# A ternary feedforward stage: its first bias as a product of four rounded rows, row scales for four tiles at once, x kept in SBUF, and longer lags in each engine's order

## The reference, cut to what matters

```python
def rms_norm(x): return x * rsqrt(mean(x * x, -1) + EPS)
def act_quant(x):
    scale = 127.0 / clip(max(abs(x), -1), 1e-05)
    return clip(round(x * scale), -128.0, 127.0) / scale
def weight_quant(w):
    scale = 1.0 / clip(mean(abs(w)), 1e-05)
    return clip(round(w * scale), -1.0, 1.0) / scale
def bitlinear158(x, w, b):
    return act_quant(rms_norm(x)) @ weight_quant(w).T + b
h = silu(bitlinear158(x, w1, b1))      # 2048 x 2048
h = gelu(h)                            # the exact form
h = layer_norm(h, ln_g, ln_b)
x = layernorm(x + bitlinear158(h, w2, b2))
```

## Time and profile before

| | |
|---|---|
| Median of three runs | 2302.09 us (2299.7 to 2304.48) |
| Span of the profiled execution | 2297.3 us |
| Stage `ternary_feedforward` in it | from about 1976.6 us to the end |
| Busy over the whole span | PE 81%, DVE 65%, ACT 41%, POOL 23% |
| Mean granted TensorE clock | 0.902 of full |

### The profile page before, as it was taken

The page is one execution under the profiler, slowest core; times in us unless marked ns, Lnnn a source line. Parts: engine busy times, 40 slices in busy tenths (PEclk is TensorE's granted clock), DMA queues, the critical chain, the costliest instruction groups (busy, mean ns, idle before and its releaser), DMA issues. The chain is left out here.

```text
span 2297.3 us, 32982 instructions
## 1 busy us (share of the span) xinstructions
PE 1871.9 (81%) x12321; PEld 1405.0 (61%) x12321; DVE 1483.0 (65%) x2816; ACT 941.1 (41%) x1589; POOL 520.8 (23%) x515
## 2 busy tenths in 40 slices
PE   2337989874667999999999959999984998478886
PEld 2225555521446999999999948787763776234443
DVE  8846877577673665666566645657662776467775
ACT  1004555620322444444444433333434111477774
POOL 0032322045010001010000001100100887234442
PEclk9958999965888999999999979999987999789897
DMA  5089999323742222212222232322214113600100
GB/s 201 0 125 144 142 142 140 48 101 121 227 140 70 61 65 59 81 58 66 74 74 64 60 108 102 111 74 74 100 57 177 49 48 105 243 10 28 37 14 23
DMA packets 145837, 208.45 MB, mean 91 GB/s; under 512 B 13520, under 2 KB 84048, under 8 KB 143248
## 3 DMA queue, kind: packets, MB, share of 16 engines
q1 hardware_dynamic: 136720, 189.57, 31.8%
q10 hardware_dynamic: 8960, 16.78, 1.9%
HBM read 159.82 MB, written 46.22 MB: 90 GB/s over the span
## 5 line engine op out<-in xcount | busy, mean ns | idle before, releaser
L452 DVE TENSOR_REDUCE a_rowmax<-a_ring 128x2 f32<-128x512 f32 x256 | 164.9, 687 | 82.6 <-PE a_ring L534 80.6
L1594 DVE TENSOR_TENSOR f_hid<-f_gate,f_gu 128x256 f32<-128x256 f32 x264 | 108.3, 420 | 162.1 <-ACT f_gate L1466 159.4
L1466 ACT ACTIVATE f_gate<-f_gu 128x256 f32<-128x256 f32 x264 | 98.7, 382 | 274.5 <-PE f_gu L1332 187.2
L2431 PE MATMUL e_py<-e_kv,e_toep 128*128 128x320 f32 x640 | 174.9, 437 | 4.7 <-DVE e_kv L2455 4.7
L397 ACT ACTIVATE a_prob<-a_sT 128x1024 f32<-128x1024 f32 x128 | 130.6, 1026 | 74.1 <-PE a_sT L523 73.7
L2431 PEld LDWEIGHTS e_py<-e_kv,e_toep 128*128 128x128 f32 x640 | 122.9, 192 | 56.5 <-issue 6.5
L1345 PE MATMUL f_gu<-f_lowh,f_bg 128*128 128x256 f32 x704 | 141.3, 283 | 5.3 <-POOL f_lowl L1251 5.0
L1332 PE MATMUL f_gu<-f_xhi,f_wg 128*128 128x256 f32 x704 | 129.8, 282 | 0.0
L1332 PE MATMUL f_gu<-f_xhi,f_wu 128*128 128x256 f32 x704 | 129.1, 281 | 0.0
L1345 PEld LDWEIGHTS f_gu<-f_lowh,f_bg 128*128 128x128 f32 x704 | 115.8, 191 | 9.8 <-POOL f_lowl L1251 5.2
L1599 DVE TENSOR_TENSOR f_hl<-f_hid,f_hh 128x768 fp32r<-128x768 f32 (+2 forms) x90 | 84.7, 941 | 55.9 <-ACT f_hh L1512 54.8
(11 more groups left out here) (379 smaller groups left out, 4967.5 us busy)
## 6 DMA issues: line engine op xcount, KB each, us to landing
f_entry<-in_WdT SPq DMA_DIRECT2D x89, 256.0 KB, 2.8
d_staging<-in_w SPq DMA_DIRECT2D x16, 1024.0 KB, 5.5
a_qs<-parts SPq DMA_DIRECT2D x96, 128.0 KB, 6.3
a_ks<-parts SPq DMA_DIRECT2D x96, 128.0 KB, 6.9
parts<-a_hi SPq DMA_DIRECT2D x16, 512.0 KB, 8.7
parts<-a_lo SPq DMA_DIRECT2D x16, 512.0 KB, 8.9
e_toep<-lags SPq DMA_DIRECT2D x32, 256.0 KB
f_entry<-in_Bg SPq DMA_DIRECT2D x89, 64.0 KB, 1.8
```

The source lines that it names most:

```text
L452: dve.tensor_reduce(rowmax[:, s % 2, :, e * SLOTS + j], ring[n % RING][:, :].rearrange("p (q t) -> p q t", t=T), AX.X, ALU.max, negate=Tru ...
L1466: act.activation(gate[:, i % 2, :], gu[n % 3][:, 0, :], ACT.Silu).then_inc(s_["gate_ready"], 1)
L1594: dve.tensor_tensor(hid[:, j, :], gate[:, i % 2, :], gu[n % 3][:, 1, :], ALU.mult).then_inc(s_["hid_ready"], 1)
L2431: last = pe.matmul(py[n % RING][:, 0:DIAG * BS], toep[:, h % 3, (t - j) * P:(t - j + 1) * P], kv[:, h % 2, :, j, :], start=(j == 0), stop= ...
```

## The change: what it does, and the diff

- The bias of the first product: b1 is loaded on 4 partitions. ACT and DVE split it once into a rounded fp32r part and its remainder (`g_bhigh`, `g_bpart`). The number per row is split likewise into four columns (`g_lcols`), which PE transposes to four rows (`g_lrows`, through `g_pq1` and an ACT copy, once for four tiles). The bias is then a product of 4 rows by 512 columns in fp32r, four matmuls per tile, in place of the 128-row fp32 product. `g_diag` is gone.
- Row maxima, roots and scales of x are made for a group of four tiles at once: `group_peaks`, `group_scales`, four squares in a row on ACT, one root on POOL.
- x is loaded by SP in four transfers of four tiles and stays in SBUF. The ring and its refills are gone.
- `g_hc` has four buffers instead of two. Steps run from -3 to 23 instead of 0 to 22.
- The order of PE in a step: bias and matmuls of W(s-1); the transposed rows of a group (at s = -1, 3, 7, 11); q(s); the four transposed groups of tile s-5; O(s-6).
- The order of ACT in a step: squares of four tiles of x (at s = -3, 1, 5, 9); the copy of `g_lrows` (at s = -1, 3, 7, 11); on even s silu(s-1), `g_q1f`(s), gelu(s-2), on odd s gelu(s-2), `g_q1f`(s), silu(s-1); squares about the mean (s-3); four `g_q2f` copies (s-5); squares of `g_hc` (s-4).
- The order of DVE in a step: scales of a group; mean and gain product (s-3), no longer behind the squares about the mean; addition and statistics (s-7); scales and rounding of `g_hc` (s-5); `g_xq`(s); shift and maximum of `g_hc` (s-4); result (s-7); maxima of a group.
- The order of POOL in a step: root of a group of x; root of s-5; root of s-7; b2 added to x (s-1); root of s-3.

```diff
-    DEPTH = 6
+    GT = 4
+    NG = NT // GT
     QB = INNER // 512
-    XT = 8
+    LAST = 8
+    STEPS = range(-3, NT + LAST)
...
+    def group_at(s, lead):
+
+        t = s + lead
+        return t // GT if 0 <= t < NT and t % GT == 0 else None
...
+        lcols = mk.sb("g_lcols", [P, NT, 4])
+        lrows = mk.sb("g_lrows", [4, 2, GT * P], F32R)
...
-        hc = mk.sb("g_hc", [P, 2, INNER])
+        hc = mk.sb("g_hc", [P, 4, INNER])
...
+                def load_x(g):
+                    sp.dma_start(xt[:, tiles(g), :], io["x5"][g * GT * P:(g + 1) * GT * P, :].rearrange("(n p) f -> p n f", p=P)
+                                 ).then_inc(got_x[g], 16)
...
+                load_x(1)
...
+                        pool.wait_ge(s_["ssq2"], t + 1)
+                        root(row2[:, t, :], 0, INNER, s_["root2"])
+                    t = tile_at(s, 7)
+                    if t is not None:
+                        pool.wait_ge(s_["var_ready"], t + 1)
+                        root(stats[:, t, :], 7, 1.0, s_["root_ready"])
+                    t = tile_at(s, 1)
+                    if t is not None:
+                        pool.wait_ge(s_["q1_ready"], t + 1)
+                        if t == 0:
+                            pool.wait_ge(s_["b2_in"], 16)
+                        pool.tensor_tensor(xt[:, t, :], xt[:, t, :], b2[:, :], ALU.add).then_inc(s_["b2_added"], 1)
+                    t = tile_at(s, 3)
                     if t is not None:
...
                 for s in STEPS:
-                    t = tile_at(s, 4)
+                    g = group_at(s, 3)
+                    if g is not None:
...
+                        if g == 0:
+                            act.wait_ge(s_["b1_in"], 16)
+                            act.activation(bhigh[:, :], brow[:, :], ACT.Copy).then_inc(s_["bhigh_ready"], 1)
+                    g = group_at(s, 1)
+                    if g is not None:
+                        act.wait_ge(s_["turned"], turn_at["f", g] + 1)
+                        if g >= 2:
+                            act.wait_ge(s_["h_done"], (g - 1) * GT)
+                        act.activation(lrows[:, g % 2, :], pq1[0:4, :], ACT.Copy).then_inc(s_["turn_read"], 1)
+                    for first, lag in ((True, 1), (False, 2)) if s % 2 == 0 else ((True, 2), (False, 1)):
+                        t = tile_at(s, lag)
+                        if t is not None:
+                            silu(t) if lag == 1 else gelu(t)
+                        t = tile_at(s, 0) if first else None
+                        if t is not None:
+                            act.wait_ge(s_["turned"], turn_at["q", t] + 1)
+                            if t >= 2:
+                                act.wait_ge(s_["h_done"], t - 1)
+                            act.activation(q1f[:, t % 2, :, :], pq1[:, :].rearrange("p (k t) -> p k t", k=KT), ACT.Identity,
+                                           bias=minus[:, :]).then_inc(s_["turn_read"], 1)
+                    t = tile_at(s, 3)
...
                 for s in STEPS:
                     t = tile_at(s, 1)
                     if t is not None:
-                        pe.wait_ge(s_["q1_ready"], t + 1)
-                        if t >= 1:
-                            pe.wait_ge(s_["q1f_ready"], t)
...
                         if t >= 1:
                             pe.wait_ge(s_["silu_done"], t)
                         else:
                             pe.wait_ge(s_["got_w1"], 16 * KT)
+                            pe.wait_ge(s_["bpart_ready"], 1)
+                        pe.wait_ge(s_["turn_read"], turn_at["q", t] + 1)
                         for n in range(QB):
-                            pe.matmul(p1[:, n * 512:(n + 1) * 512], diag[:, t % 2, :], b1[:, n * 512:(n + 1) * 512],
-                                      start=True, stop=False)
+                            pe.matmul(p1[:, n * 512:(n + 1) * 512], lrows[:, t // GT % 2, t % GT * P:(t % GT + 1) * P],
+                                      bpart[:, n * 512:(n + 1) * 512], start=True, stop=False)
+                        for n in range(QB):
+                            for j in range(KT):
+                                last = pe.matmul(p1[:, n * 512:(n + 1) * 512], q1f[:, t % 2, j, :], w1[:, j, n * 512:(n + 1) * 512],
+                                                 start=False, stop=(j == KT - 1))
+                        last.then_inc(s_["h_done"], 1)
+                    g = group_at(s, 1)
+                    if g is not None:
+                        pe.wait_ge(s_["lift_ready"], g + 1)
+                        claim(("f", g))
+                        for i in range(GT):
+                            last = pe.transpose(pq1[0:4, i * P:(i + 1) * P], lcols[:, g * GT + i, :], keep["ident"][:, :])
+                        last.then_inc(s_["turned"], 1)
+                    t = tile_at(s, 0)
+                    if t is not None:
+                        pe.wait_ge(s_["q1_ready"], t + 1)
+                        claim(("q", t))
+                        for j in range(KT):
+                            last = pe.transpose(pq1[:, j * P:(j + 1) * P], xq[:, t % 2, j * P:(j + 1) * P], keep["ident"][:, :])
+                        last.then_inc(s_["turned"], 1)
                     t = tile_at(s, 5)
...
-                    t = tile_at(s, 5)
+                    t = tile_at(s, 6)
...
+                    of = tiles(g)
+                    dve.wait_ge(s_["root1"], g + 1)
+                    dve.wait_ge(s_["max1"], g + 1)
+                    xs.step(dve.tensor_tensor(top[:, of], peak[:, of], xroot[:, of], ALU.mult))
+                    xs.step(dve.tensor_scalar(top[:, of], top[:, of], 1e-5, None, ALU.max))
+                    dve.tensor_scalar(back1[:, of], top[:, of], 1 / 127.0, wmean[:, 0:1], ALU.mult, ALU.mult).then_inc(s_["x_steps"], 1)
+                    xs.n += 1
+                    xs.step(dve.reciprocal(inv1[:, of], top[:, of]))
+                    dve.scalar_tensor_tensor(fore1[:, of], inv1[:, of], 127.0, xroot[:, of], ALU.mult, ALU.mult
+                                             ).then_inc(s_["fore_ready"], 1)
+                    xs.step(dve.tensor_scalar(lift[:, of], inv1[:, of], wfac[:, :], None, ALU.mult))
+                    xs.step(dve.tensor_copy(lhigh[:, of], lift[:, of]))
+                    high = lhigh[:, of].bitcast(F32)
+                    dve.tensor_copy(lcols[:, of, 0:2], high.unsqueeze(2).broadcast_to([P, GT, 2])).then_inc(s_["x_steps"], 1)
+                    xs.n += 1
+                    xs.step(dve.tensor_tensor(lcols[:, of, 2:4], lift[:, of].unsqueeze(2).broadcast_to([P, GT, 2]),
+                                              high.unsqueeze(2).broadcast_to([P, GT, 2]), ALU.subtract))
+                    dve.sem_inc(s_["lift_ready"], 1)
...
                 for s in STEPS:
-                    t = tile_at(s, 1)
+                    g = group_at(s, 2)
+                    if g is not None:
+                        group_scales(g)
+                    t = tile_at(s, 3)
                     if t is not None:
+                        dve.wait_ge(s_["gelu_done"], t + 1)
+                        dve.tensor_scalar(hs[:, t, 1:2], hs[:, t, 0:1], -1.0 / INNER, None, ALU.mult).then_inc(s_["mean_ready"], 1)
...
+                        dve.scalar_tensor_tensor(hc[:, t % 4, :], ha[:, t % 3, :], hs[:, t, 1:2], gain[:, :], ALU.add, ALU.mult
+                                                 ).then_inc(s_["gained"], 1)
+                    t = tile_at(s, 7)
                     if t is not None:
...
+                    t = tile_at(s, 0)
+                    if t is not None:
+                        dve.wait_ge(s_["fore_ready"], t // GT + 1)
+                        if t >= 2:
+                            dve.wait_ge(s_["turned"], turn_at["q", t - 2] + 1)
+                        dve.tensor_scalar(xq[:, t % 2, :], xt[:, t, :], fore1[:, t:t + 1], ROUND, ALU.mult, ALU.add
+                                          ).then_inc(s_["q1_ready"], 1)
...
+                    g = group_at(s, 3)
+                    if g is not None:
+                        group_peaks(g)
+                        if g == 0:
+                            dve.wait_ge(s_["bhigh_ready"], 1)
+                            dve.scalar_tensor_tensor(bpart[:, :], bhigh[:, :].bitcast(F32), takes[:, 1:2], brow[:, :],
+                                                     ALU.mult, ALU.add).then_inc(s_["bpart_ready"], 1)
```

More of the change, by code:

```diff
@@ L2506, in ternary_feedforward, with tile_at @@
     NT = N // P
-    DEPTH = 6
+    GT = 4
+    NG = NT // GT
     QB = INNER // 512
-    XT = 8
+    LAST = 8
+    STEPS = range(-3, NT + LAST)
     own = keep["ternary"]
     wmean, winv = own["wmean"], own["winv"]
+    def tile_at(s, lag):
+        t = s - lag
+        return t if 0 <= t < NT else None
+    def group_at(s, lead):
+        t = s + lead
+        return t // GT if 0 <= t < NT and t % GT == 0 else None
+    turn_at = {}
+    for s in STEPS:
+        if group_at(s, 1) is not None:
```

(31 more changed lines are left out.)

176 lines of the change are left out of this document (75 added, 101 removed).

## The result

The changed kernel takes 2344.8 us (median of four runs, 2342.21 to 2345.81), the kernel before 2301.44 us beside it (four runs, 2299.7 to 2304.48): a ratio of 1.0176, 95% interval [1.0161, 1.0192]. It is 1.8% slower. The forecast was 2351. The profiled execution has a span of 2342.6 us against 2297.3, and a mean granted clock of 0.888 against 0.902.

A forecast was written before the change was run, and what follows sets the result against it. No engine was full; a chain of waits through PE and ACT bound the kernel. W(5) to W(15) +35, start +3 and end +11 made +49 on 2297.3: span 2346, median 4.8 higher, 2351 us; range 2332 to 2372.

The forecast's parts named there:

- The ring: W(5) to W(15): each step one closed loop of PE's and ACT's parts, 33.7 us per two tiles against 34 before.
- The clock: PE behind its idle stretch runs transposes and O at half clock, adding 2.7 us per step.
- The bias: On PE, four fp32r matmuls at 0.93 us per tile replace bias passes of 9.7 us per two tiles.
- The rival of a dear one: Four-row fp32r bias matmuls run as the old passes, 2.7 us more in ten steps: 2378 us, chance 0.05.
- The port: POOL's addition of b2 holds up DVE and makes `g_xq` late: 1.0 us per odd step, hidden in even ones.
- Four tiles at once: ACT's `g_lrows` copy costs 2 us each in steps 7 and 11, 4 in all; squares and group scales nothing.
- The start: Loads and first tiles up to the end of W(5): +3 us, from -4 to +10.
- The end: From W(15) to the end of the span: about 77 us instead of 66.2, +11, between 2 and 14.
- The rival "each engine at its own busy time": Transposes do not hold PE; each engine runs at its busy time, 12.9 us per tile: 2270 us, chance 0.07.

The follow-up runs named there:

- e3: The changed kernel with the four bias matmuls of each tile done four times; 2407.18 us, ratio 1.0444 to the kernel before.
- e1: The changed kernel with O(s-6) ahead of the transposed groups of tile s-5 in PE's order; 2306.7 us, ratio 1.0008 to the kernel before.
- e5: The changed kernel with PE making the second transposed group fourteen times for tiles 1 to 11; 2324.1 us, ratio 1.0102 to the kernel before.
- e7: e1 with DVE making `g_xq`(s) right behind the gain product and POOL's addition of b2 last; 2309.09 us, ratio 1.0032 to the kernel before.
- e2: The changed kernel with PE making the second transposed group ten times for tiles 1 to 11; 2336.31 us, ratio 1.0129 to the kernel before.
- e6: The changed kernel with POOL's addition of b2 last in a step, behind the root of s-3; 2345.52 us, ratio 1.0189 to the kernel before.
- e9: e8 with PE making the second transposed group six times for tiles 1 to 11; 2277.49 us, ratio 0.9881 to the kernel before.
- e8: e7 with ACT's `g_lrows` copy behind gelu and DVE's split of b1 behind the first group scales; 2300.21 us, ratio 0.9994.
- e4: The kernel before, its order kept, with b1 and `g_diag` rounded to fp32r and the low part left out; 2289.3 us, ratio 0.9928.

## Why the prediction was right, point by point

- **The ring** held. It was forecast that W(5) to W(15) becomes one closed loop of PE's and ACT's parts, 204.5 us; it took 200.2. e3 shows that PE's work lies in it undiminished, and e1 that O is what was put in series: 29.7 us of the ten tiles go with it, clock included. Each part fits too: from W's end to the third group the sum has 8.5 us for an even step (7.8 and the first copy), and all five take 8.5. PE's idle time ahead of the third group was to be 5.3 and 6.7 us and is 5.7 to 7.2; ACT's even chain was to be 7.8 and is 7.75 (2071.04 to 2078.79).
- **The clock** was right in kind and too large in size: 2.7 per step, measured 2.1 (after against e5, 1.3 to 2.8). The transposes lose 0.74, where 0.9 was forecast, and O the other 1.3, where 1.8 was; O was sized by the slow rows of the tail, mean 5.44, and took 3.8 to 5.3 in the loop (15 of its 16 matmuls), since PE regained full speed within it. The Trainium skill's rule on recurring idle stretches ("TensorE: Matmul & The Clock Gate", "HAM oscillation — how this bites in real kernels") agrees with after, where every round starts slow behind 5.7 to 7.2 us of idle. The shorter stretches do not fit so simply: in e7 and e2, behind 2.3 and 2.5 us, the transposes could still run at full speed (1.23) and the slow work came behind them, and behind 1.8 us in the next step of e2 none came.
- **The bias** starts the next block 1.13 us later, not 0.93: 4-row fp32r matmuls of 512 columns stand 0.28 apart. Over ten tiles that is 2 us too little in the sum. The rival of a dear one fell.
- **The port** was right: 1.50 instead of 0.48, 1.0 in DVE's queue. In the ring it is worth 0.7 to 1.1 in the three odd steps where nothing hides it (e6), 1.0 was forecast. In the Trainium skill this is the exclusive lock of "SBUF — State Buffer", "🔬 SBUF: two separate sides", and POOL's 2.24 with DVE's 1.50 fit it.
- **Four tiles at once**: the `g_lrows` copy was to cost 2 in two odd steps. The third group starts 9.4 us behind W's end there and 7.8 in steps 13 and 15: 1.6 each. The four squares of x, put at nothing, cost 1.0 in step 9 (8.8 us): POOL's root for a tile of `g_hc` stands behind the group's root, which needs these squares, so the rounding on DVE starts 0.9 us late, and q waits 1.57 us instead of 0.52.
- **The start** was the weak point, as said: +3 forecast, +7.6 within the stage. Counted from the stage's start, W(0) ends as forecast, W(2) 1.4 us late, W(4) 3.5 and W(5) 4.8 (the sum had 88.0 us to there, the trace 92.8; its +3 set this against 85.3). So most of the miss comes before W(4). There bias and W run slow in W(1) (2.06 and 6.02) and W(3) (2.07 and 5.11), and W alone in W(4) (5.09 for 15), and the sum for the start had no slow products. The step from W(4) to W(5), 24.9 us, was forecast at 23.6, but its long wait has a cause that was put at nothing: at s = 5 the four squares of x stand ahead of POOL's root for tile 0, DVE waits 6.07 us for that root, and PE 8.14 for q(5), whose `g_xq` stands behind. In e7, which makes `g_xq` first, this step takes 21.0 us (e1: 25.1). The slow products of the start are read from the trace only; no run took them apart.

```profile
2051.48 0.21 DVE L2792 TENSOR_SCALAR g_row<-g_row 128x1 f32<-128x1 f32 x1 [6.07 <-POOL g_row L2614]
2054.21 1.11 PE L2737 MATMUL g_pq<-ident,g_xq 128*128 128x128 f32 x4 [8.14 <-DVE g_xq L2840]
```

- **The end**: +11 forecast, +5.2 measured. Steps of the tail are 11.7 us apart (2281.35 to 2328.07 is four of them) instead of 12.6, because O there took 3.4 to 4.8 us and not 5.4. The same size was off as in the loop.

```profile
2281.35 4.73 PE L2758 MATMUL g_pout<-g_w,g_q2f 128*128 128x512 bf16 x15 [0.22 <-issue]
...
2304.89 3.40 PE L2758 MATMUL g_pout<-g_w,g_q2f 128*128 128x512 bf16 x15
...
2328.07 3.57 PE L2758 MATMUL g_pout<-g_w,g_q2f 128*128 128x512 bf16 x15 [0.22 <-issue]
```

So the span was forecast 3.6 us too long, with the start 6.2 too short including the stage's later beginning, and loop and end 10 too long: part of the accuracy is errors that met. Another 2.6 came from the median, which stood 2.2 above the span this time and not 4.8: the timed runs lie some 1.8 us above their own span, so 3.0 of the 4.8 was a profiled execution of the kernel before that happened to be fast, no property of the kernel. The stated range is not the sum of its bounds either: 1.5 to 3.3 us per step, -4 to +10 for the start and 2 to 14 for the end add up to 2323 to 2367, not 2332 to 2372. 2344.8 lies in both.

The rival "each engine at its own busy time" (12.9 us per tile) was wrong for this kernel, whose PE waits in the third group; e9, which shortens that wait to between 0 and 1.6 us, comes to 14.7.

## What to carry to other kernels

Where one engine works through several tiles in one program, look at each wait in the middle of it and at what stands behind: a product that is ready must not stand behind a wait for another tile. Count a step as the closed chain through all engines, not by the busiest one; and on TensorE read the granted clock behind each idle stretch, since a wait that is shortened may be paid back by slow matmuls. Before an order is judged, run it once with TensorE kept busy by harmless repeats: it separates what the order costs from what the clock takes, and may be the version to keep.

## What was not expected of the hardware

- Useless transposes made the kernel faster: 2300.2 to 2277.5 us with 20 more per tile (e8, e9), 2344.8 to 2324.1 with 52 more (e5).
- Half clock does not need long idle stretches here. After 2.3 us of waiting and 1.2 us of transposes at full speed, bias and W ran slow (e7: 1.66 and 6.04 us), while in the kernel before half clock followed waits of about 4 us. What decides between the two cases of e2 (2.54 us slow, 1.81 us not) stays open. The length of the wait alone does not: in e9 a wait of 1.56 us (2080.56) was followed by a W of 3.63 us, and one of 1.57 (2109.45) by a W of 5.32.
- Four-row fp32r matmuls cost as much per column as those of 128 rows: 1.20 us for four on 4 rows, 1.17 on 128 (e4).
